# Hard graph attention: values by column tiles, no own-head step, scores by head on 32 by 32 tiles

## The reference

```python
Q, K, V = x @ WQ.T, x @ WK.T, x @ WV.T          # each split in 8 heads of 32
energy = Q @ we.T + be
attn = einsum('hqd,hkd->hqk', Q, K) * SCALING + energy
attn = softmax(attn + where(adj > 0, 0.0, -inf))
hard = (attn == max(attn, axis=-1, keepdims=True)) / HEADS
out = einsum('hqk,hkd->hqd', hard, V)
return layernorm(x + out)
```

## Time and profile before

| | |
|---|---|
| median of three runs | 1510.71 us |
| the profiled execution | 1505.37 us, its span 1503.6 us |
| PE matmul busy | 1185.0 us (79%), 11346 records |
| DVE busy | 1055.1 us (70%), 3140 instructions |
| ACT busy | 830.9 us (55%) |
| POOL busy | 739.0 us (49%) |
| DMA | mean 193 GB/s |
| mean granted TensorE clock | 0.929 |

### The profile page before, as it was taken

One profiled execution on the slowest core, in us unless ns is written; L12 is line 12 of the kernel. 1 busy time (PEld: TensorE's weight loads), 2 busy tenths in 40 slices (PEclk: granted clock), 3 DMA queues, 4 the chain that ended last, 5 costly groups with the idle time before them and its releaser, 6 DMA issues.

```text
span 1503.6 us, 45448 instructions
## 1 busy us (share of the span) xinstructions
PE 1185.0 (79%) x11346; PEld 899.7 (60%) x11347; DVE 1055.1 (70%) x3140; ACT 830.9 (55%) x1515; POOL 739.0 (49%) x820
## 2 busy tenths in 40 slices
PE   5779588888888888888878787887887888788881
PEld 3334366676666666666667566665665666666661
DVE  4445377777777777777777677777777777777772
ACT  1422365675656655665566465656565656664551
POOL 0000555666666655566555554554454545455550
PEclk9989799999999999899899999989999989999996
DMA  4732577665756666756675666656666676665561
GB/s 143 241 127 97 184 258 216 183 213 185 241 158 224 194 205 199 215 180 204 209 223 160 193 220 192 218 197 199 230 220 214 199 247 199 198 205 157 171 179 42
DMA packets 87215, 290.88 MB, mean 193 GB/s; under 512 B 14688, under 2 KB 27744, under 8 KB 87200
## 3 DMA queue, kind: packets, MB, share of 16 engines
q0 software_dynamic: 48720, 199.60, 42.7%
q1 hardware_dynamic: 38480, 91.11, 17.7%
HBM read 275.97 MB, written 14.68 MB: 193 GB/s over the span
## 4 chain that ended last, share of the span: by engine, by line
DVE 34%; issue 23%; PE 16%; DVEq 12%; DMA 11%; ACT 2%; POOL 1%; POOLq 0%; ACTq 0%; SPq 0%
DMA kv<-kv_table,picks 9%; DVE best L769 8%; DVE reached L741 4%; DVE picks L759 4%; PE ps_s L929 3%; DVE hit L747 3%; PE ps_o L1022 3%; DVE o_run L783 3%; PE ps_s L1010 2%; DVE minus_top L772 2%; PE ps_s L991 2%; DVEq L281 2%; PE ps_s L919 2%; DMA be_sb<-in_L_gnn_be 1%; DVEq L279 1%
## 5 line engine op out<-in xcount | busy, mean ns | idle before, releaser
L398 POOL DMA_INDIRECT kv<-kv_table,picks x609 | 584.6, 960 | 468.9 <-PE ps_o L1022 300.7
L991 PE MATMUL ps_s<-k_t,q_blk 128*128 128x384 f32 x804 | 364.2, 536 | 0.0
L490 ACT ACTIVATE hard<-ps_s,minus_top 128x384 bf16<-128x384 f32 x402 | 211.3, 577 | 234.6 <-DVE minus_top L772 230.2
L389 POOL TENSOR_TENSOR q_blk<-q_t,minus_same 128x256 f32<-128x256 f32 x202 | 152.9, 757 | 262.9 <-issue 157.3
L485 ACT COPY k_t<-ps_s 128x384 f32<-128x384 f32 x404 | 176.2, 483 | 184.5 <-PE ps_s L1010 183.0
L1010 PE MATMUL ps_s<-ident_f,kv 128*128 128x128 f32 x1212 | 184.7, 293 | 88.0 <-DMA kv<-kv_table,picks 81.7
L1022 PE MATMUL ps_o<-kv,hard_t 124*128 124x128 bf16 x3600 | 248.4, 226 | 0.1
L769 DVE TENSOR_REDUCE best<-ps_s 128x1 f32<-128x384 f32 x402 | 204.6, 550 | 36.4 <-PE ps_s L993 19.7
L1022 PEld LDWEIGHTS ps_o<-kv,hard_t 124*128 124x128 bf16 x3600 | 224.5, 102 | 6.2 <-issue 2.7
L475 ACT ACTIVATE hard_t<-ps_h 128x768 bf16<-128x768 bf16 x200 | 162.0, 810 | 112.6 <-PE ps_h L1002 111.9
L783 DVE SCALAR_TENSOR_TENSOR o_run<-o_run,keep,ps_o 128x128 f32<-128x128 f32 x400 | 120.7, 343 | 130.0 <-issue 96.2
(11 more groups left out here) (135 smaller groups left out, 1319.5 us busy)
## 6 DMA issues: line engine op xcount, KB each, us to landing
adj_in<-in_adj SPq DMA_DIRECT2D x128, 512.0 KB, 8.8
kv_table<-kv_out SPq DMA_DIRECT2D x32, 320.0 KB, 2.5
kv<-kv_table,picks POOLq DMA_INDIRECT x609
x_in<-in_x SPq DMA_DIRECT2D x8, 512.0 KB, 7.3
x_row<-in_x SPq DMA_DIRECT2D x32, 128.0 KB
out<-y_out SPq DMA_DIRECT2D x32, 128.0 KB
w<-in_L_gnn_WQ SPq DMA_DIRECT2D x1, 256.0 KB, 3.1
w<-in_L_gnn_WK SPq DMA_DIRECT2D x1, 256.0 KB, 6.1
```

The lines of the kernel that those rows point to most:

```text
L398: pool.indirect_dma_start(kv[m % RING][:, c, :], None, kv_table, bass.IndirectOffsetOnAxis(ap=picks[m % RING][:, c, 2:3], axis=0)).then_in ...
L490: done = act.activation(hard[m % 2][:, h, :], ps_s[m % 2][h][:, 0:SLOTS], ACT.Sign, bias=minus_top[m % 2][:, h:h + 1], scale=-1.0)
L991: pe.matmul(bank[:, 0:SLOTS], q_blk[m % 2][:, h, :], k_t[m % 2][:, h, :], start=True, stop=False)
```

## The change

Five things are changed together.

1. The table holds values by head: for each head its three parts side by side, 96 columns (`v_part`, `by_head`).
2. `values` multiplies each head's 32 queries by that head's 96 columns alone: for each half and chunk four matmuls with 32 stationary columns (rows of the output 32 j), 24 of them in place of 18. The output is 128 by 96 for each half.
3. `own_heads` goes on DVE and PE, and `own_rows` on ACT. The running output is kept for eight groups (`o_all`), and `merge` addresses the group's part by a register (`groups`). After four groups DVE transposes their part in 32 by 32 blocks (`turn_rows`), and `rows_back` sums the three parts with six fp32 matmuls, whose right side holds 1/8 and, for the second half, is rotated by a block. The branch on the end of a group becomes a count.
4. POOL copies the group's queries as they are (`q_now`, 64 columns, four buffers); the sign moves to `query`.
5. `scores` is one matmul per head, 32 deep, 32 wide, 384 columns, fp32: four for a half, and both halves one after the other, after all six mask matmuls of the item (`beyond`). The second half's heads lie one block of rows further. `hards_across(b)` follows behind both halves.

```diff
-        def v_part(k, i): return kv_out[k % GT][:, D:ROW].bitcast(BF16)[:, i * D:(i + 1) * D]
+        def v_part(k, i): ....rearrange("p (h i c) -> p h i c", h=H, i=PARTS)[:, :, i, :]
...
-        def group_ended(eng, r):
-            return eng.If_ne(bits_of(eng, r["began"], 1), 0)
+        def count_groups(eng, r):
+            eng.reg_add(r["groups"], r["groups"], bits_of(eng, r["began"], 1))
...
-            def blocks_of_q(m, due):
-                    wait_alone(pool, pe_score[1], due(pe_score[1], -2))
-                pool.tensor_tensor(q_blk[m % 2] ..., q_t[...] broadcast, minus_same ..., ALU.mult)
+            def queries(m, due):
+                    wait_alone(pool, pe_score[1], due(pe_score[1], -RING))
+                pool.tensor_copy(q_now[m % RING][:], q_t[:, :, bass.ds(at, GQ)]).then_inc(q_made, 1)
...
-            def merge(m, due):
-                dve.wait_ge(pe_pv, due(pe_pv))
+            def merge(m, due, group):
+                width = PARTS * HD
                 dve.wait_ge(dve_keep, due(dve_keep))
                 for h in range(HALVES):
-                    done = dve.scalar_tensor_tensor(out=o_run[:, h, :], in0=o_run[:, h, :], ...,
-                                                    in1=ps_o[:, h * P:(h + 1) * P], ...)
+                    o_run = o_all[:].rearrange(...)[:, bass.ds(group * (HALVES * width) + h * width, width)]
+                    done = dve.scalar_tensor_tensor(out=o_run, in0=o_run, ...,
+                                                    in1=ps_o[:, h * width:(h + 1) * width], ...)
+                    if h == 0:
+                        done._wait_ge(pe_pv, due(pe_pv))
...
-            def own_heads(m, due):
-                dve.wait_ge(dve_merge, due(dve_merge))
-                dve.tensor_tensor(o_own[:], o_run[:], same[:].unsqueeze(1).to_broadcast([P, HALVES, P]), ALU.mult)
+            def turn_rows(at, merged):
+                dve.wait_ge(dve_merge, merged)
+                dve.transpose(o_t[:].rearrange("p k (g q) -> p g k q", g=GPT),
+                              o_all[:, at:at + GPT, :].rearrange("p g (k c) -> p g k c", c=HD))
...
-                    with group_ended(dve, r):
-                        own_heads(b - 1, for_loop(dve, r, -1))
-                        dve.reg_add(r["groups"], r["groups"], 1)
+                    if b == 0:
+                        with rows_due(dve, r):
+                            odd = bits_of(dve, r["te_done"], 1)
+                            with dve.If_lt(odd, 1):
+                                turn_rows(0, ...)
+                            with dve.If_ne(odd, 0):
+                                turn_rows(GPT, ...)
+                    count_groups(dve, r)
...
-                    merge(b, for_loop(dve, r, 0))
+                    merge(b, for_loop(dve, r, 0), dve.snap(r["groups"]) & (2 * GPT - 1))
...
-            def scores(m, due, h): (one matmul q_blk x k_t, then three mask matmuls)
+            def beyond(m, due): (the six mask matmuls, the first of each chunk with start)
+            def scores(m):
+                for h in range(HALVES):
+                    for i in range(HEADS4):
+                        head, row = slice(i * HD, (i + 1) * HD), (i + h) % HEADS4 * GQ
+                        mm = pe.matmul(ps_s[m % 2][h][row:row + GQ, 0:SLOTS], q_now[m % RING][head, h, :],
+                                       k_t[m % 2][head, h, :], start=False, stop=True)
+                    mm.then_inc(pe_score[h], 1)
...
-                        for i in range(PARTS):
-                            v = i * D + h * P
-                            mm = pe.matmul(ps_o[:, h * P:(h + 1) * P], hard_t[m % 2][0:USED, at:at + P], ...)
+                        for j in range(HEADS4):
+                            row, v = j * GQ, (h * HEADS4 + (j - h) % HEADS4) * PARTS * HD
+                            mm = pe.matmul(ps_o[row:row + GQ, h * PARTS * HD:(h + 1) * PARTS * HD],
+                                           hard_t[m % 2][0:USED, at + row:at + row + GQ], ...)
...
                 for b in range(RING):
                     planes_of(b + 4, ...)
-                    scores(b + 1, for_loop(pe, r, 1), 0)
+                    beyond(b + 1, for_loop(pe, r, 1))
+                    scores(b + 1)
+                    walk()
                     hards_across(b, for_loop(pe, r, 0))
-                    scores(b + 1, for_loop(pe, r, 1), 1)
-                    walk()
```

More of the change, by code:

```diff
@@ L152, in hard_attention @@
         kv = [sb(f"kv{i}", [P, CHUNKS, ROW], F32) for i in range(RING)]
-        q_blk = [sb(f"q_blk{i}", [P, HALVES, P], F32) for i in range(2)]
+        q_now = [sb(f"q_now{i}", [P, HALVES, GQ], F32) for i in range(RING)]
         k_t = [sb(f"k_t{i}", [P, HALVES, SLOTS], F32) for i in range(2)]
@@ L408, in _ @@
                     next_item(pool, r)
[L409 removed]
+                    queries(m, None)
                 gather(m, for_item(m))
@@ L492, in hards @@
                 done.then_inc(act_hard, 1)
-            def own_rows(tiles):
-                act.wait_ge(pe_own, tiles * GPT + 1)
-                act.wait_ge(pe_y, tiles)
-                act.copy(o_t[:].rearrange("p a q -> p (a q)"), own_t).then_inc(act_own, 1)
             def row_std(te):
@@ L535, in turn @@
                     hards(b + 1, for_loop(act, r, 1))
-                    with group_ended(act, r):
-                        act.reg_add(r["groups"], r["groups"], 1)
-                        with act.If_lt(bits_of(act, r["groups"], 3), 1):
-                            own_rows(act.snap(r["groups"]) >> 2)
+                    count_groups(act, r)
                     if b == 0:
@@ L563, in _ @@
             dve.memset(one[:], 1.0)
-            dve.memset(o_run[:], 0.0)
+            dve.memset(o_all[:], 0.0)
             dve.memset(minus_top[1][:], 0.0)
@@ L984, in planes_of, with beyond @@
                 mm.then_inc(pe_planes, 1)
-            def scores(m, due, h):
-                if h == 0:
-                    pe.wait_ge(q_made, due(q_made))
-                    pe.wait_ge(act_masked, due(act_masked))
-                bank = ps_s[m % 2][h]
-                pe.matmul(bank[:, 0:SLOTS], q_blk[m % 2][:, h, :], k_t[m % 2][:, h, :], start=True, stop=False)
-                for c in range(CHUNKS):
-                    mm = pe.matmul(bank[:, c * P:(c + 1) * P], masked[m % RING][:, c, :, :].rearrange("p h q -> p (h q)"),
-                                   mask_of[:], start=False, stop=(c == CHUNKS - 1))
-                mm.then_inc(pe_score[h], 1)
+            def beyond(m, due):
+                pe.wait_ge(q_made, due(q_made))
+                pe.wait_ge(act_masked, due(act_masked))
+                for h in range(HALVES):
+                    for c in range(CHUNKS):
+                        pe.matmul(ps_s[m % 2][h][:, c * P:(c + 1) * P],
+                                  masked[m % RING][:, c, :, :].rearrange("p h q -> p (h q)"),
+                                  mask_of[:], start=(c == 0), stop=False)
+            def scores(m):
+                for h in range(HALVES):
+                    for i in range(HEADS4):
[3 more added lines that the diff above has]
+                    mm.then_inc(pe_score[h], 1)
             def hards_across(m, due):
@@ L1019, in values, with rows_back @@
                         at = (h * CHUNKS + c) * P
-                        for i in range(PARTS):
-                            v = i * D + h * P
-                            mm = pe.matmul(ps_o[:, h * P:(h + 1) * P], hard_t[m % 2][0:USED, at:at + P],
-                                           kv[m % RING][0:USED, c, D:ROW].bitcast(BF16)[:, v:v + P],
-                                           start=(c == 0 and i == 0), stop=(c == CHUNKS - 1 and i == PARTS - 1))
+                        for j in range(HEADS4):
+                            row, v = j * GQ, (h * HEADS4 + (j - h) % HEADS4) * PARTS * HD
+                            mm = pe.matmul(ps_o[row:row + GQ, h * PARTS * HD:(h + 1) * PARTS * HD],
+                                           hard_t[m % 2][0:USED, at + row:at + row + GQ],
+                                           kv[m % RING][0:USED, c, D:ROW].bitcast(BF16)[:, v:v + PARTS * HD],
+                                           start=(c == 0), stop=(c == CHUNKS - 1))
                 mm.then_inc(pe_pv, 1)
-            def own_heads():
-                at = ((pe.snap(r["groups"]) + 3) & 3) * GQ
+            def rows_back(te):
+                pe.wait_ge(dve_turned, te + 1)
                 for h in range(HALVES):
-                    mm = pe.matmul(own_t[:, bass.ds(at + h * P, GQ)], o_own[:, h, :], pick_q[:], start=True, stop=True)
-                    if h == 0:
-                        mm._wait_ge(dve_own, r["groups"])
-                mm.then_inc(pe_own, 1)
-            def rows_back(te):
-                pe.wait_ge(act_own, te + 2)
-                for h in range(HALVES):
-                    mm = pe.transpose(ps_y[:, h * P:(h + 1) * P], o_t[:, h, :], ident_f[:])
```

(11 more changed lines are left out.)

63 lines of the change are left out of this document (28 added, 35 removed).

## The result

The changed kernel took **1586.01 us** (median of 4 runs, 1583.31 to 1588.17) beside 1509.83 us for the kernel before (4 runs, 1508.32 to 1512.88): ratio 1.0501, 95% interval 1.0477 to 1.0525. It is 5% slower. The forecast was 1478 us with a chance of 0.49 for faster: the direction was wrong, while the time lies in the range 1450 to 1600.

The account below looks back on a forecast made before the run. DVE, with its sequencer, was taken to bound the loop, PE second by about 12%. Terms -40 - 36 - 7 + 40 + 30 - 20 + 1 = -32 us gave 1478 us, range 1450 to 1600.

Parts of the forecast that it names:

- PE in the new order must stay beneath this: PE's loop work, some 1130 us against DVE's 1277, stays second; scores 0.7 to 1.4 us a step.
- rival 1: PE's score matmuls: fp32 pairs queue up, 3.1 us a step, PE becomes the bound; 1560 us, chance 0.30.
- DVE waiting at `tops`: Sign of a wrong forecast: DVE waits there for the scores, with score matmuls over 2.5 us or more.
- rival 2: PE's score tiles: four heads writing one PSUM bank do not overlap, 5.6 us a step; about 2050 us, chance 0.08.
- score matmuls spread over more than 2.5 us: Sign on PE of a wrong forecast, 2.5 us or more a step; less than 1.5 us would show it right.
- Address of the merge: DVE ahead of merge: the group's address in a register costs 0.20 us an item, +40 us (+20 to +70).
- DVE's own program: DVE in the loop: apart from a true wait of 20 us at L689, all is its own work, 1277 us.
- Own heads, branch, merge's width, transposes: DVE: own heads and branch removed -40 us, narrower merge -7, turning the rows +30, constants and memset +1.
- wait at L689: DVE's `pay` waiting for step 0's values: new PE order, narrower values and earlier row turning save 20 us (0 to -20).
- POOL and DVE on one port: POOL's smaller query copy stretches DVE's `owners`, `bits` and `own_heads` less: -36 us, between 0 and -51.
- Rival 3: DVE's gains taken back by POOL's copy, address 0.35 us, transpose 1.6 us: 1500 to 1550, likeliest 1510; chance 0.14.
- The clock: PE may lose clock, 0.95 in the loop before, with less to do; matters only if DVE then waits for it.

Follow-up runs that it names:

- third set: Changed kernel, tile scores alone and tile scores with their own rows rerun unchanged beside the kernel before (1497.75 us); changed kernel 1503.81 us, 1.0037.
- first comparison: The complete change against the kernel before, the study's original measurement: 1586.01 us beside 1509.83 us, ratio 1.0501.
- the second: Set with the changed kernel rerun unchanged and three variants, beside the kernel before (1508.29 us); changed kernel 1590.12 us, 1.0528.
- fifth set: Changed kernel rerun unchanged and plain loads, beside the kernel before (1514.28 us); changed kernel 1602.47 us, 1.0581.
- plain loads: Changed kernel with each indirect gather replaced by a plain load of as many bytes, always the same table rows; 1495.37 us, 0.9956; again 1494.54 us, 0.9877.
- fourth set: Changed kernel and values alone rerun, with and without a fixed address, beside the kernel before (1500.56 us); changed kernel 1506.31 us, 1.0033.
- values alone with a fixed address: Values alone, merging always into the first group's place (groups' sums mixed), against the kernel before; 1511.63 us, 1.0030; again 1477.95 us, 0.9846.
- score tiles alone: Kernel before with tile scores, second half's own-heads mask turned to match; 1691.82 us, 1.1212; again 1477.53 us, 0.9872.
- tile scores alone: Kernel before with only the tile scores and their order, own-heads mask not turned (heads mixed); 1469.16 us, 0.9785; again 1472.03 us, 0.9834.
- values alone: Changed kernel with query block, scores and their order as before (heads mixed), against the kernel before; 1536.22 us, 1.0235; again 1533.40 us, 1.0224.

## Why the prediction was wrong

**The measured 76 us.** The step that failed is "PE in the new order must stay beneath this". It compares PE's amount of work with DVE's and takes each engine's result to reach the next when it is done, so it adds nothing for ACT's wait for `hards_across`. This wait measured 524 us (112 before, 183 in the unheld changed kernel of the third set), and the circle of values, gathers, held completion and `hard_t`, 6.5 us an item, took the path from DVE. The direction failed through the held completions, which are no term of the sum and no rival. That 1586 us lies in the range is luck: its upper part was there for rival 1. In the three sets with them (the first comparison, the second and the fifth set) the changed kernel is at 1.050, 1.053 and 1.058; in the two without, at 1.0037 and 1.0033. So of the +76, +82 and +88 us, 70 to 83 come and go with the held completions, and some +5 are the change itself. What they need: the gathers' indirect issue (the plain loads end them) and something of the set of runs (the same files show both). A chip of one and the same number had the changed kernel free of them in the fourth set and held in the fifth, so the number of the chip doesn't explain it. In profiles that have them, the trace is short of semaphore records as well, 14,900 to 16,300 for 19,600 to 20,000. The plain loads of the fifth set have all theirs (19,738). The missing ones are of POOL, DVE, ACT and the DMAs (45 of 204 are left of `q_now`'s in the first profile), hardly any of PE, whose semaphores are the late ones. Each kernel lost something else in such a set: the kernel before 0.7% (1508 to 1514 us for 1498 to 1501), value tiles alone 1.9% (1.0030 for 0.9846, with the fixed address), both tiles some 5%, score tiles alone 13.6% (1.1212 for 0.9872). So it isn't the count of short matmuls, which is highest with both tiles. In the last the circle is longer: full values take 1.18 us for 0.44, and the gathers start 1.95 us behind their start for 1.23. No profile of the kernel before was taken in such a set, so why it is spared is open.

The Trainium skill (NOTIFIC — the notification-queue block, 7.1 Overflow: three behaviours, one of which stalls the engine) states that the block that writes out records pushes back on the engines when its internal pipeline fills. The same section says that this push-back loses no record, and that records are dropped, in one of its modes, when a queue's ring in memory is full, so it doesn't by itself account for both signs here, missing records and late completions. Every run timed here has a span and a clock, so some recording was on in each, and no run was made without it. Whether a kernel that isn't recorded is held stays open. The Trainium skill (DMA: Bandwidth & Descriptors, SWDGE vs HWDGE vs iDMA) adds that GpSimd writes descriptors into SBUF for the DMAs issued from it, direct and indirect. Which part of the indirect issue matters here, no run shows.

**Rival 1** named a time that came near (1560) and a sign that appeared (DVE waiting at `tops`, 41.5 us), but its mechanism is wrong. The sixteen score instructions of an item are recorded in 0.87 us at full clock: eight first passes 7 ns apart, and the second passes 0.34 us behind them. Where completions aren't held, the semaphore comes 0.11 us behind. The fp32 pairs don't queue up, nor do four heads in one bank wait for each other (rival 2). A time that fits a rival is no proof of it: its own sign, score matmuls spread over more than 2.5 us, was absent in the first profile, where they spread over 1.5 us at most.

**The sum, where nothing is held,** was to be -32 us and is +5. Point by point:

- *Address of the merge*: +40 forecast, **+55** measured. I took the second half's address to hide beneath the first; it pushes back the sequencer's work behind the merge, 0.12 us an item. "DVE's own program" of the earlier trace rows includes the sequencer, and what is put into it anywhere shows up.
- *Own heads, branch, merge's width, transposes*: -40 - 7 + 30 + 1 = -16, and with the wait at L689 -36; the values alone with a fixed address measure 0.9846, -23 us. The transposes were right: 0.978 us each for 0.96. `bits` to `best` is 0.266 us (median) in the unheld changed kernel for 0.26, but 0.453 us in the values alone with a fixed address, where POOL's multiply is still there: part of this gain only comes with the next one.
- *POOL and DVE on one port*: -36, as part of the tile scores alone. These measure 0.9785, 0.9834 and 0.9872, that is -19 to -32. `reached` and `bits` came down to 0.319 and 0.259 us, where 0.31 and 0.26 were forecast, while with POOL's multiply kept (the values alone with a fixed address) they take 0.380 and 0.383 us: the rows below, in this order. So the mechanism was right, and somewhat less of it reaches the end.
- *Wait at L689*: -20. Worked out as in the forecast, in the unheld changed kernel it is 23.2 - 10 x 1.5 = 8 us, so 12 of 20 are gone (in the fourth set 12.7 - 6 x 1.5 = 4 us); with the tile scores alone it is 60.2 - 20 x 1.5 = 30 us, more than before. That kernel has the new order and the values alone don't, and there it is 12.4 - 5 x 1.5 = 5 us. So the reason given, that the new order takes 0.7 us off the way to the values, isn't borne out: the wait is smaller in the kernels with the narrower values and the turning of the rows ahead of it, whatever the order.

```profile
L728 DVE TENSOR_SCALAR reached<-iota_h,ends_of 128x384 bf16<-128x384 f16 x199 | 63.5, 319 | 0.0
L748 DVE TENSOR_TENSOR bits<-picks,bit 128x96 uint32<-128x96 uint32 x199 | 51.6, 259 | 6.8
```
```profile
L751 DVE TENSOR_TENSOR bits<-picks,bit 128x96 uint32<-128x96 uint32 x200 | 76.6, 383 | 6.8
L731 DVE TENSOR_SCALAR reached<-iota_h,ends_of 128x384 bf16<-128x384 f16 x200 | 75.9, 380 | 0.0
```
The waits at L689 (L676, L687 and L679 in these kernels; us, times, longest) in the changed kernel of the third set, the tile scores alone and the values alone of the first:
```profile
DVE pay L676 <- PE ps_o L1022: 23.2, 10, 3.4
```
```profile
DVE pay L687 <- PE ps_o L1026: 60.2, 20, 5.4
```
```profile
DVE pay L679 <- PE ps_o L1019: 12.4, 5, 3.4
```

The parts add up: values +34, tile scores -19 to -32, together +2 to +15, measured +5. Against the forecast's -32 us the address gives 15 of the 37 us of the miss; the rest is in the port, in L689 and in own heads, and isn't separated further. A likely part of it, which no run isolates: "all else is DVE's own program" was too strong, since the chain before has DMA for 11% and PE for 16%, and where a gather ends the step, time saved on DVE doesn't reach the end. Rival 3 (DVE's gains taken back, +5 us at half of its departures) has the unheld kernel's time, 1504 and 1506 us, but not its conditions: POOL's copy doesn't stretch DVE as before, the address costs 0.27 us for its 0.35, and a transpose 0.98 us for its 1.6.

**The clock** isn't the cause. It was granted at 0.80 in the held loop and at 0.84 in the unheld one, both down from 0.95; with 0.84 the loop is as long as before, and the plain loads of the fifth set, at 0.85 over the whole run, are 108 us faster than the kernel beside them at 0.80. The forecast said that it matters only if DVE then waits, and that holds.

**A better version**: tile scores with their own rows, values and own heads as before, took 1477.53 us (0.9872) where nothing is held, and 1691.82 (1.1212) where completions are. Of the kernels here that compute the reference's output, only the kernel before has kept its time, to about 1%, in both kinds of set.

## What to carry to other kernels

An engine whose busy time leaves gaps may still be bound by its sequencer: an address from a register costs there, 0.27 us for the two of an item, even if the instruction itself is shorter; price it by what it pushes back, also behind the instruction. Before a profile is explained by the kernel, run the unchanged kernel again in another set: here 5 to 14% lay in the set and was first read as the kernel's. The kernels with tile matmuls beside indirect DMAs of GpSimd lost 2 to 14% in such a set, the one with full-size matmuls alone 0.7%; why, stays open.

## What was unexpected of the hardware

- A matmul's recorded end and its semaphore can be 1 to 3 us apart while GpSimd issues indirect DMAs, with DVE's and ACT's semaphores prompt beside them. The releaser then reads "remote" or "another core or an unknown queue", and the recorded durations look innocent.
- Tiles: eight 32 by 32 fp32 matmuls on eight tiles, four of them writing other partitions of the same bank, started 7 ns apart and took 0.87 us with their second passes. The Trainium skill (TensorEngine Tiling (Array Packing), Gotcha 1: PSUM Pressure) says that different row tiles cannot access one bank simultaneously; the measurement differs and decides. Twenty-four value tiles took 0.44 us, where I had 0.6.
- The three gathers of an item take 3.5 us of POOL as indirect ones (0.957 us each) and 1.6 us as plain ones (0.537 us each), yet with nothing held this moves the time by under 1%.
